# Products over a tile of ones at the start, an earlier load of the first keys, and mask rows loaded from the sixth turn on

## What is computed

```python
x = x + attn_a(layernorm(x))   # 16 heads of 8, rotary positions, softmax over all 256 keys
x = x + ffn(layernorm(x))      # silu(x Wg) * (x Wu), hidden 384, then Wd; integer weights / 127
x = x + attn_b(layernorm(x))   # 16 heads of 8, causal, sparsemax instead of softmax
x = x + ffn(layernorm(x))      # the same weights as before
```

## Time and profile before

| What | Value |
|---|---|
| median of 3 executions | 613.9 us (612.51 to 620.14) |
| profiled execution, its own time | 616.62 us |
| its span, first to last instruction | 614.8 us |
| mean granted clock of TensorE | 0.985 of full |
| TensorE matmuls busy | 574.9 us (94%) |
| TensorE weight loads busy | 443.4 us (72%) |
| VectorE busy | 487.5 us (79%) |
| ScalarE busy | 422.7 us (69%) |
| GpSimd busy | 386.1 us (63%) |
| chain that ended last | TensorE 69%, VectorE 15%, "issue" 6%, ScalarE 3%, DMA 3% |

### The profile page before, as it was taken

How to read it: one execution, slowest core, us unless ns; L and a number is a source line. 1 busy time by engine, 2 the same in 40 slices (tenths; PEclk the granted TensorE clock), 3 DMA queues, 4 the chain that set the end, 5 groups by cost and what they waited for, 6 DMA issues and landing times.

```text
span 614.8 us, 19033 instructions
## 1 busy us (share of the span) xinstructions
PE 574.9 (94%) x6646; PEld 443.4 (72%) x6646; DVE 487.5 (79%) x1426; ACT 422.7 (69%) x1057; POOL 386.1 (63%) x819
## 2 busy tenths in 40 slices
PE   5888989999999999999999999999899999999883
PEld 4555546777677777767677888788788888888663
DVE  3599858889888888987787888888888888989432
ACT  1115647777877777788887777777677777777772
POOL 4755555676776667677666766676666666663332
PEclk9899979999999999999999999999999999999998
DMA  8656655676566654555445444432644445450000
GB/s 219 178 148 166 167 138 132 150 170 157 140 159 155 136 144 126 140 129 135 132 117 135 125 123 117 109 98 55 163 107 112 117 116 126 125 125 13 20 11 21
DMA packets 74656, 76.24 MB, mean 124 GB/s; under 512 B 10348, under 2 KB 68908, under 8 KB 70092
## 3 DMA queue, kind: packets, MB, share of 16 engines
q1 hardware_dynamic: 63636, 68.09, 43.1%
q10 hardware_dynamic: 10920, 6.88, 5.2%
HBM read 46.86 MB, written 23.33 MB: 114 GB/s over the span
## 4 chain that ended last, share of the span: by engine, by line
PE 69%; DVE 15%; issue 6%; ACT 3%; DMA 3%; SPq 2%; POOL 1%; ACTq 0%; POOLq 0%; DVEq 0%
PE banks L1537 15%; PE banks L1491 10%; PE banks L1515 9%; PE banks L1404 7%; PE banks L1465 7%; DVE top L1109 4%; PE banks L1456 3%; PE banks L1494 2%; DVE neg_shift L1103 2%; DVE top L1108 2%; PE banks L1436 2%; PE banks L1457 2%; ACT probs_t L1300 2%; PE banks L1414 2%; PE banks L1518 1%
## 5 line engine op out<-in xcount | busy, mean ns | idle before, releaser
L1300 ACT ACTIVATE probs_t<-banks 128x512 f32<-128x512 f32 (+1 forms) x512 | 267.4, 551 | 79.6 <-PE banks L1515 51.9
L1103 DVE TENSOR_REDUCE neg_shift<-banks 128x2 f32<-128x512 f32 x256 | 166.0, 681 | 38.0 <-PE banks L1491 36.8
L1537 PE MATMUL banks<-probs_t,v_ext 128*32 128x256 f32 (+1 forms) x2048 | 118.5, 361 | 0.0
L1491 PE MATMUL banks<-k_stack,q_stack 72*128 72x256 bf16 x512 | 100.5, 278 | 8.1 <-issue 4.4
L1109 DVE MAX8 top<-banks 128x8 f32<-128x256 f32 x256 | 106.0, 414 | 0.0
L1515 PE MATMUL banks<-q_stack,k_stack 75*128 75x256 bf16 x512 | 100.0, 277 | 0.3 <-ACT probs_t L1300 0.2
L980 POOL TENSOR_TENSOR hidden<-up_tanh,gate_half 128x256 f32<-128x256 f32 x96 | 69.9, 731 | 42.6 <-DVE up_tanh L1149 42.3
L1108 DVE MAX8 top<-banks 128x8 f32<-128x128 f32 x256 | 74.3, 290 | 26.1 <-PE banks L1500 25.2
L1537 PEld LDWEIGHTS banks<-probs_t,v_ext 128*32 128x32 f32 x2048 | 55.7, 110 | 38.7 <-issue 13.9
L1491 PEld LDWEIGHTS banks<-k_stack,q_stack 72*128 72x128 bf16 x512 | 40.8, 98 | 48.2 <-DVE neg_shift L1103 34.4
L1494 PE MATMUL banks<-k_stack,q_stack 128*128 128x128 bf16 x256 | 56.6, 221 | 7.5 <-DVE top L1109 5.0
(11 more groups left out here) (113 smaller groups left out, 1369.4 us busy)
## 6 DMA issues: line engine op xcount, KB each, us to landing
q_stack<-q_image SPq DMA_DIRECT2D x93, 192.0 KB
k_stack<-k_image SPq DMA_DIRECT2D x93, 192.0 KB
q_image<-qk_parts SPq DMA_DIRECT2D x32, 192.0 KB, 2.3
k_image<-qk_parts SPq DMA_DIRECT2D x32, 192.0 KB, 2.1
q_image<-qk_parts SPq DMA_DIRECT2D x32, 128.0 KB, 2.2
o_image<-out_t SPq DMA_DIRECT2D x32, 128.0 KB, 1.8
out_compact<-o_image SPq DMA_DIRECT2D x32, 64.0 KB
rdenominators<-r_image SPq DMA_DIRECT2D x16, 128.0 KB, 2.4
```

Of the source, the lines that this page charges most:

```text
L1103: dve.tensor_reduce(m.nm[:, n % STACKS, h, :], scores.rearrange("p (q k) -> p q k", q=TT), AX.X, ALU.max, negate=True).then_inc(reduced, 1)
L1300: act.activation(m.pt[:, (n * Q + g) % GROUPS, i, 0:size], shifted_banks[:, j % 2, 0:size], ACT.Exp if is_soft(n) else ACT.Relu, scale=SCA ...
L1491: ins = pe.matmul(scores[:, qt * T:(qt + 1) * T], qs[0:STACK, h, qt * P:(qt + 1) * P], ks[0:STACK, h, :], start=True, stop=True)
L1537: ins = pe.matmul(out_bank[32 * i:32 * i + 32, at + skip:at + T], v_windows(v, kt)[:, Q * g + i, :], m.pt[:, (n * Q + g) % GROUPS, i, kt * ...
```

## The change

Four edits. `WARM_UP`: ahead of all its other work TensorE waits for the memset of `one_rows` (48 partitions of ones, set by GpSimd) and makes 24 products of 48 rows by 128 and 256 columns with it, into the bank that `spare` uses. `SPARE`: 46 spare products in place of 34 at step -16, 10 in place of 12 at step -10. The loads of item 0: the first half of the keys is issued right behind the first half of the queries, and the other halves of both follow (`load_other_heads`). The mask rows: the eight calls of `load_mask_rows` stand at the fourteenth step of turns 5 to 12 (steps 93, 109, ... 205) in place of the tenth of turns 3 to 10.

```diff
--- before.py
+++ after.py
@@ -70,7 +70,8 @@
 X_REST = {-22: (3, 5), 1: (5, 8), 27: (8, 12), 43: (12, 16)}
 
 
-SPARE = {-16: 34, -10: 12}
+WARM_UP = 24
+SPARE = {-16: 46, -10: 10}
 SPARE_SCORES = 3
 SPARE_END = 29
 
@@ -794,15 +795,11 @@
                 r = n % STACKS
                 sp.wait_ge(q_stored, (n + 1) * (2 * SEM))
                 wait(sp, shifted_ready, (n - STACKS + 1) * H)
-                first = H // 2 if n == 0 else 0
-                for rep in range(PARTS if n == 0 else 0):
-                    rows = slice(rep * PARTS * HD, (rep + 1) * PARTS * HD)
-                    sp.dma_start(m.qs[r][rows, 0:first, :], q_rows[rep * HD:(rep + PARTS) * HD, 0:first])\
-                      .then_inc(first_q_loaded, SEM)
+                first, last, loaded = (0, H // 2, first_q_loaded) if n == 0 else (0, H, q_loaded)
                 for rep in range(PARTS):
                     rows = slice(rep * PARTS * HD, (rep + 1) * PARTS * HD)
-                    sp.dma_start(m.qs[r][rows, first:H, :], q_rows[rep * HD:(rep + PARTS) * HD, first:H])\
-                      .then_inc(q_loaded, SEM)
+                    sp.dma_start(m.qs[r][rows, first:last, :], q_rows[rep * HD:(rep + PARTS) * HD, first:last])\
+                      .then_inc(loaded, SEM)
                 if not is_soft(n):
                     sp.dma_start(m.qs[r][STACK:SHIFTED, :, :], m.zero_rows[:, :]).then_inc(q_loaded, SEM)
 
@@ -810,13 +807,19 @@
                 r = n % STACKS
                 sp.wait_ge(k_stored, (n + 1) * SEM)
                 wait(sp, shifted_ready, (n - STACKS + 1) * H)
-                first = H // 2 if n == 0 else 0
-                for rep in range(PARTS if n == 0 else 0):
-                    rows = slice(rep * PARTS * HD, (rep + 1) * PARTS * HD)
-                    sp.dma_start(m.ks[r][rows, 0:first, :], k_rows[0:PARTS * HD, 0:first]).then_inc(first_k_loaded, SEM)
+                first, last, loaded = (0, H // 2, first_k_loaded) if n == 0 else (0, H, k_loaded)
                 for rep in range(PARTS):
                     rows = slice(rep * PARTS * HD, (rep + 1) * PARTS * HD)
-                    sp.dma_start(m.ks[r][rows, first:H, :], k_rows[0:PARTS * HD, first:H]).then_inc(k_loaded, SEM)
+                    sp.dma_start(m.ks[r][rows, first:last, :], k_rows[0:PARTS * HD, first:last]).then_inc(loaded, SEM)
+
+            def load_other_heads():
+                for rep in range(PARTS):
+                    rows = slice(rep * PARTS * HD, (rep + 1) * PARTS * HD)
+                    sp.dma_start(m.qs[0][rows, H // 2:H, :], q_rows[rep * HD:(rep + PARTS) * HD, H // 2:H])\
+                      .then_inc(q_loaded, SEM)
+                for rep in range(PARTS):
+                    rows = slice(rep * PARTS * HD, (rep + 1) * PARTS * HD)
+                    sp.dma_start(m.ks[0][rows, H // 2:H, :], k_rows[0:PARTS * HD, H // 2:H]).then_inc(k_loaded, SEM)
 
             def load_shift(n):
                 wait_freed(sp, "shift", n)
@@ -882,6 +885,8 @@
                     load_out(n)
                 if (n := due(step, "load_k")) is not None:
                     load_k(n)
+                    if n == 0:
+                        load_other_heads()
                 if (n := due(step, "store_rden")) is not None and is_soft(n):
                     store_rden(n)
                 if (n := due(step, "load_rden")) is not None and is_soft(n):
@@ -1347,8 +1352,8 @@
                        .then_inc(x_rest_loaded[x_piece(first)], SEM)
                 if step == ONCE["bulk"]:
                     load_weights()
-                n, j = divmod(step - 3 * H, H)
-                if 0 <= n < 2 * STACKS and j == 9:
+                n, j = divmod(step - 5 * H, H)
+                if 0 <= n < 2 * STACKS and j == 13:
                     load_mask_rows(*divmod(n, 2))
                 if (n := due(step, "take_out")) is not None:
                     take_out(n)
@@ -1552,6 +1557,9 @@
                 pe.matmul(out_bank[:, D:2 * D], m.wb[:, WB["bvc"]:WB["bvc"] + D], m.wb[:, WB["o"]:WB["o"] + D],
                           start=True, stop=True).then_inc(bias_summed, 1)
 
+            pe.wait_ge(ones_set, 1)
+            for i in range(WARM_UP):
+                pe.matmul(shifted_banks[:, 1, 0:T], m.one_rows[:, 0:P], m.one_rows[:, :], start=True, stop=True)
             pe.wait_ge(ident_cast, 1)
             for step in range(FIRST_STEP, LAST_STEP):
                 n, h = divmod(step, H)
```

## The result

The changed kernel takes 610.96 us, median of 20 executions (608.22 to 615.21); the kernel before takes 618.1 in as many (612.43 to 624.1). The ratio is 0.991, with a 95% interval from 0.9886 to 0.9935. That is 5.6 us less (4.0 to 7.0), where 6.3 were forecast, and it is clear of no change. The ratio leaves out every execution more than 1.5% above the fastest of its kernel (four of the kernel before, none of the changed one), while the two medians of all twenty differ by 7.1 us. The time itself was forecast as 607.6 us and is 3.4 over that. The profiled execution has a span of 607.8 us against 614.8. The scatter of the executions got smaller too, from 11.7 to 7.0 us between the lowest and the highest, and that turns out to be a part of the story.

A forecast was written before the change was run, and what follows sets the result against it. TensorE was taken as full nearly throughout, leaving gains only in the head, near 84 us and in the clock. 5.6 + 0.7 = 6.3 us gave 610.3 for the profiled execution, 607.6 as median; range 603.5 to 612.

The forecast's parts named there:

- I take 0 for them: Head: the 24 products over 48 rows of ones were taken not to lift the clock, gain 0.
- Cost taken: 0: Turns 5 to 12: the moved mask rows delay no item's first scores; up to 1.9 us a turn otherwise.
- rival D: Turns 5 to 12: moved mask rows make first scores late by up to 1.9 us each; 617.2 us, chance 0.04.
- Rival C: Item 4's key load is late from other loads ahead on SyncE's queue; clock still falls; 612.7 us, chance 0.10.
- Within 2%: 0.92: Whole kernel: chance 0.92 that the time lands within 2%, 12.3 us, taken as not told from no change.
- The median of the three runs is 613.9, 2.7 below it: 607.6.: Whole kernel: level of the forecast, set 2.7 us below the 610.3 reckoned from the profiled execution.
- A: Head: products over ones lift the clock before 7.42 us, giving 2.6 us instead of 0.7; 605.7 us, chance 0.27.
- Part 1: Item 4's key load: moving the mask rows shortens the wait and avoids the clock's fall, 5.6 us gained.
- Its price: Behind item 4's wait: the clock's fall cost 3.1 to 4.1 us over eight steps, taken as 3.6.
- Part 2: Head: three edits bring items 0 and 1 earlier; 0.7 us of gain kept.
- From there 0.7 us are left: Item 1: its keys come 0.7 to 0.8 us earlier, its wait grows to 1.8 us, and 0.7 us is kept.
- Rival B: Before item 1's scores: the longer wait, 1.8 us, makes the clock fall, price about 3.6 us; 611.2 us, chance 0.11.

The follow-up runs named there:

- e3_ones_128: Changed kernel with the 24 starting products over 128 rows of ones in place of 48; 612.39 us, ratio 0.994.
- e1_masks_only: Kernel before with only the mask rows moved to step 13 of turns 5 to 12; 613.46 us, ratio 0.9933.
- after_again: The changed kernel, unaltered, profiled a second time; 611.36 us, ratio 0.9876.
- before_2: The kernel before, unaltered, profiled a second time; 17.86 us between the starts of items 2's and 3's exponentials, no total time given by name.
- e6_turn_3_step_13: Changed kernel with the mask rows at step 13 but from turn 3 on; 610.78 us, ratio 0.9898, four executions.
- after_3: The changed kernel, unaltered, profiled a third time; 611.96 us, ratio 0.9891.
- e9_late_weights: e3_ones_128 with ScalarE's four bulk loads of weights and constants at step 2 in place of -22; 615.31 us, ratio 0.9944.
- e4_no_warm_up: Changed kernel without the products over the rows of ones (WARM_UP = 0); 615.17 us, ratio 0.995.
- before_3: The kernel before, unaltered, profiled a third time; 18.37 us between the starts of items 2's and 3's exponentials, no total time given by name.
- before_4: The kernel before, unaltered, profiled a fourth time; 20.12 us between the starts of items 2's and 3's exponentials, no total time given by name.

## Why the prediction was right and where it was not

**What it called.** The direction, the size of the change (6.3 us forecast, 5.6 measured), the place (item 4's key load and the clock behind it) and how little comes from the head. That the size came out so near is in part luck: as the terms below say, 4.4 and nothing stand on average where 5.6 and 0.7 were put. "I take 0 for them" held for the products over 48 rows, and the argument from the earlier trace rows was the right one: `e3_ones_128` shows that 128 rows do lift the clock. It was thin evidence, though: the stretch at half clock around those rows also holds 3.87 us of products over 128 rows (L1537). With the spare products it held (1.99 us for item 1's projection, 1.8 forecast), though not by the step I gave: "Idle time falls from 2.11 to about 0.7" was 1.61, since they ended at 16.64 and not at 17.3 to 17.5. How safe that is stays open: the clock fell behind 1.69 us of idle time in `e1_masks_only` and held behind 1.74 in `after_again`. "Cost taken: 0" for the mask rows in turns 5 to 12 held to 0.1 us over twelve turns, so rival D fell. (The stretch from 190 to 200 us that I had shown for it holds no issue of mask rows; they stand at 185.05 and 203.05.) Rival C fell with `e1_masks_only`.

**The step that failed** is the last one: "About 2%, 12.3 us, is what a measurement of this kernel can tell from no change", and from it "Within 2%: 0.92". The change is within 2%, but it can be told from none: twenty executions of each gave an interval of 0.25% to either side, and a change of 0.9% is clear of it. A forecast of 6.3 us should have been read as "faster", and not been filed under no difference. Single executions of the kernel before scatter by 1.9% (612.43 to 624.1); that is not the resolution of a median of twenty.

The other step that failed is the level: "The median of the three runs is 613.9, 2.7 below it: 607.6." Twenty executions put the kernel before at 618.1, 4.2 above those three, and the changed one at 610.96, 3.4 above 607.6 and near the upper end of the range. The value of 610.3, reckoned from the profiled execution, would have been right within 0.7. Three executions were too few for the level. (In the chances, "faster than 601.6 needs more than A" has 0.06 where all gains beyond A have 0.03; these don't fit together.)

**Terms that were mis-sized.** Part 1: "The wait shrinks to 0.2 to 0.7; I take 0.5" was 0, so 2.5 and not 2.0 us: the load took 6.1 us at most from issue to use, not 7.0 to 7.5. The fall cost 10.74 - 7.35 = 3.4 in the eight steps that I had priced at 3.6, and 4.0 with what lies ahead of them. And 0.5 us came between items 1 and 2, where ScalarE's two issues had stood ahead of item 4's transposed input, which I had put at nothing: in `before_2` the copy of that input starts 2.2 us behind the norm, in the changed kernel 1.4, and in `e6_turn_3_step_13`, where the issues stay in turn 3 but behind the copy, 1.4 too. The sum for that one execution was 7.0 against my 5.6. But the step "Its price" took one execution for all. The fall came in two of four, and the term is 4.4 on average.

Part 2: "the first scores come at 23.0: 1.2 us gained" was 23.77 and 0.47 in the first profile, where the keys took 23.77 - 17.89 = 5.9 us from issue to use, not 4.45; in `after_again` and `after_3` it was 22.77 and 22.99, with 4.6 at most and 4.8 us. Why the keys take 4.6 us once and 5.9 another time stays open. It isn't the weights: their loads had ended ahead of 16 us, and without them the keys took 5.1 us (`e9_late_weights`). "From there 0.7 us are left" is the step that failed here: it was 0.47 at item 1 (0.35 on average) and nothing at item 2, whose own key load stands behind item 0's shift rows; the wait there grew from 0.57 to 1.16. Rival B named what then happens: the clock falls behind such a wait. I gave it as one place and 0.11; in `after_again` and `after_3` it fell, at 37.9 and 55.0, and at 52.0. The same falls are in the kernel before, so they don't count against the change; they are part of the scatter.

**What stays open.** The parts measured alone are 4.1 us for the mask rows (2.2 to 6.0) and none for the head (1.0034, 0.9989 to 1.0079), and together they gave 5.6 (4.0 to 7.0), with 7.7 and 6.8 from the six executions each of `after_again` and `after_3`. Whether there is more in the sum than in the parts, and whether the products over 48 rows do anything (`e4_no_warm_up`), these intervals can't say; no stretch of a profile shows it. Nor is it known what decides in which executions the clock falls behind a wait.

## What to carry to other kernels

A bulk transfer that is free on average is dear in the one turn in which the load behind it has no slack: look for the load that is needed soonest after its issue, and put nothing right ahead of it, in either queue. A wait of two microseconds on TensorE can cost more by the clock behind it than by itself, and not in every execution; so price a stall from several profiles, and look at the scatter of the times as well as at their median. An earlier start is worth only what the next transfer lets through: ahead of the first edit to a head, ask what all of its waits are for.

## What the runs showed of the hardware

Products over 48 rows, back to back for 5.3 us from 1.13, left the projection at 3.57 us; the same over 128 rows brought it to 1.97. From 84.10 to 94.30 us TensorE stayed at 0.50 while it was busy 9.81 of 10.20 us, mostly with scores over 72 and 75 rows; 3.87 us of it were the products with the values (L1537), which are over 128 rows, so this stretch alone doesn't show that it is the rows.

The same program took 612.13 us in an execution with a mean granted clock of 0.997 and 620.81 in one with 0.979. The place of the falls differs from one execution to the next: item 1's keys were 0.83 us late in `before_3` and 1.68 in `before_4`, item 2's 1.27 and 0.79, and the first had its fall behind item 2 and the other behind item 1, each behind its longer wait. But behind waits of 1.33 and 1.35 us ahead of item 1 the clock held, in the first profiles of the two kernels.

A load of 576 KB on SyncE's queue took 3.2 to 3.9 us to issue when ScalarE had put 424 KB of short rows out 1.4 us ahead of it, 2.6 us when the mask rows were 0.4 us ahead (`before_2` and `before_3`, turn 4), and 1.3 us when they came 2.7 us behind.
